# Node updates of a four-layer graph network: sums read over all banks, one root for two variances, a mask on one block, vector products of a fill by halves

## What is computed

```python
x = layernorm(x + mean of edge_attr_16 over the edges of each dst)
# L1: two passes with a small network on the edge attributes giving weights w
msg_s = einsum('ei,eij->ej', x[dst], wa) / 4;  msg_v = einsum('ei,eij,ec->ejc', x[dst], wb, sh1) / 4
out   = seg_mean(concat(msg_s, msg_v), src)              # 16 scalars and 4 vectors of 3 for each node
s0    = (out_s - mean) / sqrt(var + eps) * gs0 + bs0
v0    = out_v / sqrt(mean(out_v**2 over nodes, c) + eps) * gv0
msg   = (einsum(s0[dst], wa) + einsum(v0[dst] . sh1, wb) / sqrt(3)) / sqrt(20)
x     = layernorm(x + bn(seg_mean(msg, src)))
x     = layernorm(x + (leaky_relu(bn(seg_mean(x[src] @ W_e, dst) + x @ W_root + b)) + x))
x     = layernorm(x + tanh(gcn(tanh(gcn(x)))))
```

## Time and profile before

| | |
|---|---|
| median of three runs | 4055.97 us (4052.94 to 4059.43) |
| the profiled execution | 4055.89 us, its span 4054.2 us |
| TensorE busy | 3443.1 us, 85% |
| VectorE busy | 3345.4 us, 83% |
| GpSimd busy | 2800.4 us, 69% |
| ScalarE busy | 2652.3 us, 65% |

### The profile page before, as it was taken

The page is one execution under the profiler, slowest core; times in us unless marked ns, Lnnn a source line. Parts: engine busy times, 40 slices in busy tenths (PEclk is TensorE's granted clock), DMA queues, the critical chain, the costliest instruction groups (busy, mean ns, idle before and its releaser), DMA issues.

```text
span 4054.2 us, 105185 instructions
## 1 busy us (share of the span) xinstructions
PE 3443.1 (85%) x28557; PEld 2887.9 (71%) x28558; DVE 3345.4 (83%) x6593; ACT 2652.3 (65%) x3637; POOL 2800.4 (69%) x2751
## 2 busy tenths in 40 slices
PE   3559999999999699999999977778776888878887
PEld 3438888888888477777777766777775777757775
DVE  7789999999999688888888887888886787767876
ACT  2149999999999599999999960000002566745665
POOL 4447777777777377777777747776653777657774
PEclk9999999999999799999999988777776999989999
DMA  6011111111111321111111111111111222222221
GB/s 80 27 16 24 24 26 24 24 24 26 24 24 25 22 29 31 29 31 31 31 29 31 31 22 30 30 27 27 25 20 22 45 43 42 40 34 44 44 40 29
DMA packets 285654, 124.21 MB, mean 31 GB/s; under 512 B 179726, under 2 KB 260338, under 8 KB 285622
## 3 DMA queue, kind: packets, MB, share of 16 engines
q1 hardware_dynamic: 186838, 87.92, 9.4%
q0 software_dynamic: 84672, 29.47, 8.5%
q10 hardware_dynamic: 14112, 6.43, 0.7%
HBM read 121.80 MB, written 1.78 MB: 30 GB/s over the span
## 4 chain that ended last, share of the span: by engine, by line
PE 34%; issue 21%; POOL 20%; DVE 15%; DVEq 5%; DMA 3%; ACT 1%; POOLq 0%; SPq 0%; ACTq 0%
POOL gb L446 16%; PE ps L719 10%; PE ps L735 10%; PE ps L839 6%; POOL gb L436 3%; PE ps L725 2%; DVE oht L1283 2%; PE ps L633 2%; PE ps L855 2%; DVEq L284 2%; DVE oh L971 1%; DVE rest L987 1%; DMA eat<-vtab 1%; DVE xt L1099 1%; DMA gb<-table,idx 1%
## 5 line engine op out<-in xcount | busy, mean ns | idle before, releaser
L446 POOL DMA_INDIRECT gb<-table,idx x1568 | 1620.3, 1033 | 572.1 <-issue 451.3
L436 POOL DMA_INDIRECT gb<-table,idx x1078 | 1087.9, 1009 | 545.3 <-issue 453.4
L719 PE MATMUL ps<-big,oh 128*128 128x290 f32 (+1 forms) x7840 | 1264.6, 308 | 1.6 <-DVE big L1139 1.6
L719 PEld LDWEIGHTS ps<-big,oh 128*128 128x128 f32 x7840 | 1070.3, 191 | 124.9 <-DVE big L1139 2.2
L735 PE MATMUL ps<-w,ht 128*128 128x320 f32 x3136 | 1008.3, 444 | 123.9 <-DVE xt L1099 111.6
L546 ACT ACTIVATE oh<-iota_f,src_n 128x640 fp32r<-128x640 f32 x1372 | 1024.6, 815 | 0.0
L549 ACT ACTIVATE oh<-oh,ones 128x2560 fp32r<-128x2560 f32 (+1 forms) x392 | 849.6, 2167 | 12.8
L735 PEld LDWEIGHTS ps<-w,ht 128*128 128x128 f32 x3136 | 556.6, 191 | 384.4 <-DVE xt L1099 182.9
L1099 DVE TENSOR_TENSOR xt<-ps,gb 128x640 f32<-128x640 f32 x784 | 642.8, 820 | 77.0 <-PE ps L735 25.5
L599 ACT ACTIVATE rest<-rest,dst_f x1220 | 383.0, 389 | 321.0 <-PE ps L855 269.6
L1107 DVE TENSOR_REDUCE msg<-xt 128x80 f32<-128x1280 f32 (+1 forms) x392 | 580.3, 1480 | 0.0
(11 more groups left out here) (227 smaller groups left out, 2840.4 us busy)
## 6 DMA issues: line engine op xcount, KB each, us to landing
gb<-table,idx POOLq DMA_INDIRECT x2646, 2.4
eat<-in_eat SPq DMA_DIRECT2D x196, 192.0 KB, 2.4
eat<-vtab SPq DMA_DIRECT2D x98, 160.0 KB
eat<-vtab SPq DMA_DIRECT2D x49, 256.0 KB
eat<-vtab SPq DMA_DIRECT2D x98, 128.0 KB
rest<-in_edge_attr ACTq DMA_DIRECT2D x98, 64.0 KB, 1.8
idx<-in_src SPq DMA_DIRECT2D x245, 4.0 KB
idx<-in_dst SPq DMA_DIRECT2D x196, 4.0 KB
```

Source lines behind the costliest of these rows:

```text
L436: nc.gpsimd.indirect_dma_start(out=(gb if p == 2 else gr)[:, b, t, 0:tabw[p]], out_offset=None, in_=tabs[p], in_offset=bass.IndirectOffset ...
L446: nc.gpsimd.indirect_dma_start(out=gb[:, b, t, 0:tabw[p]], out_offset=None, in_=tabs[p], in_offset=bass.IndirectOffsetOnAxis(ap=idx[:, b, ...
L719: mm = nc.tensor.matmul(out, oh5[:, b, t, c * P:(c + 1) * P], big[:, b, t, 0:W], start=False, stop=False, skip_group_check=True)
```

## The change

The change has six parts. The sums after passes 0, 1 and 2 are read by instructions that span the banks, with one for the counts, one copy and one addition (two and two after pass 1, whose sums lie in two banks). The Newton step of a square root has four instructions, and the scaling of the mean in a layer norm is part of the subtraction. After pass 0 the vectors' sum of squares is taken together with the scalars' mean, and one root with 20 columns serves both variances. The mask is applied to block 24 alone. The constant factor of pass 1 is put into the inverse counts `rcs`, behind the store of the table of pass 0. In the first two steps of pass 1 the vector products are done by halves of four tiles.

```diff
@@ -492,7 +494,7 @@
             def stat_root():
-                root(sv_root[:, :], sv[:, 0:D])
+                root(sv_root[:, :], sv[:, 0:SW])
@@ -573,9 +575,7 @@
                 stat_root()
-                if l == 0:
-                    stat_root()
-                else:
+                if l == 1:
                     node_root()
@@ -764,10 +764,10 @@
                 nc.tensor.matmul(ps[:, 7, 0:32], zeros[:, 0:P], zeros[:, 0:32], start=True, stop=True).then_inc(s_accd, 1)
                 if l == 0:
-                    for k in range(3):
+                    for k in range(2):
                         partition_sum(k)
                 else:
-                    for k in range(3, 5):
+                    for k in range(2, 4):
                         partition_sum(k)
@@ -901,9 +901,8 @@
                 dve.wait_ge(s_sqo, k)
                 link(V.tensor_scalar(tmp, root, 1e-30, None, ALU.max))
                 link(V.reciprocal(tmp, tmp))
-                link(V.tensor_tensor(tmp, tmp, v, ALU.mult))
-                link(V.tensor_tensor(root, root, tmp, ALU.add))
-                link(V.tensor_scalar(root, root, 0.5, None, ALU.mult))
+                link(V.scalar_tensor_tensor(out=tmp, in0=tmp, scalar=0.5, in1=v, op0=ALU.mult, op1=ALU.mult))
+                link(V.scalar_tensor_tensor(out=root, in0=root, scalar=0.5, in1=tmp, op0=ALU.mult, op1=ALU.add))
@@ -990,8 +989,7 @@
             def layer_norm(xx):
                 link(V.tensor_reduce(r1[:, :], xx, AX.X, ALU.add))
-                link(V.tensor_scalar(r1[:, :], r1[:, :], 1.0 / D, None, ALU.mult))
-                link(V.tensor_tensor(xx, xx, bc(r1[:, :], D), ALU.subtract))
+                link(V.scalar_tensor_tensor(out=xx, in0=bc(r1[:, :], D), scalar=-1.0 / D, in1=xx, op0=ALU.mult, op1=ALU.add))
                 link(V.tensor_tensor(t2[:, :, 0:D], xx, xx, ALU.mult))
                 link(V.tensor_reduce(r1[:, :], t2[:, :, 0:D], AX.X, ALU.add))
                 roots[0] += 1
...
-            def batch_norm(xx, g, b_):
-
-                node_sum(xx, D)
+            def mask_nodes(xx):
+                last = xx[:, NB - 1, :]
+                link(V.tensor_tensor(last, last, mask[:, NB - 1:NB].broadcast_to([P, D]), ALU.mult))
+
+            def centred(xx):
                 link(V.tensor_scalar(sm[:, 0:D], ps[:, 5, 0:D], 1.0 / N, None, ALU.mult))
                 link(V.tensor_tensor(xx, xx, over_nodes(sm[:, 0:D], D), ALU.subtract))
-                link(V.tensor_tensor(xx, xx, bc(mask[:, :], D), ALU.mult))
+                mask_nodes(xx)
                 link(V.tensor_tensor(t2[:, :, 0:D], xx, xx, ALU.mult))
                 node_sum(t2[:, :, 0:D], D)
                 roots[0] += 1
                 V.tensor_scalar(sv[:, 0:D], ps[:, 5, 0:D], 1.0 / N, EPS, ALU.mult, ALU.add).then_inc(s_sqi, 1)
-                square_root(sv[:, 0:D], sv_root[:, :], sv_t[:, :], roots[0])
-                link(V.reciprocal(sv[:, 0:D], sv_root[:, :]))
+                square_root(sv[:, 0:SW], sv_root[:, :], sv_t[:, :], roots[0])
+                link(V.reciprocal(sv[:, 0:SW], sv_root[:, :]))
+
+            def scaled(xx, g, b_):
                 link(V.tensor_tensor(sv[:, 0:D], sv[:, 0:D], par[:, g, :], ALU.mult))
                 link(V.tensor_tensor(xx, xx, over_nodes(sv[:, 0:D], D), ALU.mult))
                 link(V.tensor_tensor(xx, xx, over_nodes(par[:, b_, :], D), ALU.add))
+
+            def batch_norm(xx, g, b_):
+                node_sum(xx, D)
+                centred(xx)
+                scaled(xx, g, b_)
@@ -1143,7 +1150,16 @@
                 def step(s, b, n, first):
                     prior = not (first and b == 0)
                     dve.wait_ge(gl_in[p][b][0], n * 16 * (T // 2))
-                    if l == 1:
+                    def first_vectors(h):
+                        rh = rhat[:, s, 4 * h:4 * h + 4, :]
+                        link(V.tensor_tensor(vprod[:, 4 * h:4 * h + 4, :, :],
+                                             gb[:, b, 4 * h:4 * h + 4, 0:12].rearrange("p t (j c) -> p t j c", c=3),
+                                             repeat(rh, 2, NV), ALU.mult))
+                        link(V.tensor_reduce(gb[:, b, 4 * h:4 * h + 4, 28:32], vprod[:, 4 * h:4 * h + 4, :, :], AX.X, ALU.add))
+
+                    if l == 1 and first:
+                        first_vectors(0)
+                    elif l == 1:
                         dve.wait_ge(gl_in[p][b][1], n * 16 * (T // 2))
                         rh = rhat[:, bass.ds(s, 1), :, :].rearrange("p o t c -> p (o t) c")
                         V.tensor_tensor(vprod[:, :, :, :], gb[:, b, :, 0:12].rearrange("p t (j c) -> p t j c", c=3),
@@ -1168,6 +1184,9 @@
                                     ALU.is_equal).then_inc(l_done[l], 1)
                     reduce_half(s, b, 0, first)
                     dve.wait_ge(gl_in[p][b][1], n * 16 * (T // 2))
+                    if l == 1 and first:
+                        first_vectors(1)
+                        dve.sem_inc(q_done[l], 2)
                     products_of(s, b, 2, first)
                     if l == 0:
                         vectors(s, b, 0)
...
-                    t1c = t1[:, :, :].rearrange("p (h c) f -> p h c f", c=NC)
-                    rcc = rcs[:, :].rearrange("p (h c) -> p h c", c=NC)
-                    for c in range(NC):
-                        av = ps[:, c, 0:NH * MP[0]].rearrange("p (h f) -> p h f", h=NH)
-                        link(V.tensor_scalar(rcc[:, :, c], av[:, :, MF], 1.0, None, ALU.max))
-                        link(V.tensor_copy(t1c[:, :, c, 0:MF], av[:, :, 0:MF]))
-                        link(V.tensor_tensor(t1c[:, :, c, 0:MF], t1c[:, :, c, 0:MF], av[:, :, MF + 1:2 * MF + 1], ALU.add))
+                    t1c = t1[:, :, :].rearrange("p (h c) f -> p c h f", c=NC)
+                    rcc = rcs[:, :].rearrange("p (h c) -> p c h", c=NC)
+                    av = ps[:, 0:NC, 0:NH * MP[0]].rearrange("p c (h f) -> p c h f", h=NH)
+                    link(V.tensor_scalar(rcc, av[:, :, :, MF], 1.0, None, ALU.max))
+                    link(V.tensor_copy(t1c[:, :, :, 0:MF], av[:, :, :, 0:MF]))
+                    link(V.tensor_tensor(t1c[:, :, :, 0:MF], t1c[:, :, :, 0:MF], av[:, :, :, MF + 1:2 * MF + 1], ALU.add))
                     link(V.reciprocal(rcs[:, :], rcs[:, :]))
                     link(V.tensor_tensor(rcs[:, :], rcs[:, :], mask[:, :], ALU.mult))
...
-                    batch_norm(tab[:, :, 12:MF], GS0, BS0)
+                    link(V.tensor_reduce(stat[:, 0:D], tab[:, :, 12:MF].rearrange("p q f -> p f q"), AX.X, ALU.add))
                     link(V.tensor_tensor(t2[:, :, 0:12], tab[:, :, 0:12], tab[:, :, 0:12], ALU.mult))
-                    node_sum(t2[:, :, 0:12], 12)
-                    link(V.tensor_copy(sm[:, 0:12], ps[:, 5, 0:12]))
-                    link(V.tensor_reduce(sv[:, 0:NV], sm[:, 0:12].rearrange("p (j c) -> p j c", c=3), AX.X, ALU.add))
-                    roots[0] += 1
-                    V.tensor_scalar(sv[:, 0:D], sv[:, 0:D], 1.0 / (3 * N), EPS, ALU.mult, ALU.add).then_inc(s_sqi, 1)
-                    square_root(sv[:, 0:D], sv_root[:, :], sv_t[:, :], roots[0])
-                    link(V.reciprocal(sv[:, 0:D], sv_root[:, :]))
-                    link(V.tensor_tensor(sv[:, 0:NV], sv[:, 0:NV], par[:, GV0, 0:NV], ALU.mult))
-                    link(V.tensor_copy(sm[:, 0:12].rearrange("p (j c) -> p j c", c=3), bc(sv[:, 0:NV], 3)))
+                    V.tensor_reduce(stat[:, D:MF], t2[:, :, 0:12].rearrange("p q f -> p f q"), AX.X, ALU.add).then_inc(s_str, 1)
+                    stats[0] += 1
+                    dve.wait_ge(s_sts, stats[0])
+                    link(V.tensor_reduce(sv[:, D:SW], ps[:, 5, D:MF].rearrange("p (j c) -> p j c", c=3), AX.X, ALU.add))
+                    link(V.tensor_scalar(sv[:, D:SW], sv[:, D:SW], 1.0 / (3 * N), EPS, ALU.mult, ALU.add))
+                    centred(tab[:, :, 12:MF])
+                    link(V.tensor_tensor(sv[:, D:SW], sv[:, D:SW], par[:, GV0, 0:NV], ALU.mult))
+                    link(V.tensor_copy(sm[:, 0:12].rearrange("p (j c) -> p j c", c=3), bc(sv[:, D:SW], 3)))
+                    scaled(tab[:, :, 12:MF], GS0, BS0)
                     V.tensor_tensor(tab[:, :, 0:12], tab[:, :, 0:12], over_nodes(sm[:, 0:12], 12), ALU.mult).then_inc(s_tabr, 1)
                     dve.sem_inc(s_node, 1)
+                    link(V.tensor_scalar(rcs[:, :], rcs[:, :], float(MJ) ** -0.5, None, ALU.mult))
...
-                    t1c = t1[:, :, :].rearrange("p (h c) f -> p h c f", c=NC)
-                    for c in range(NC):
-                        W5 = NH * MP[1]
-                        av = ps[:, c // 3, (c % 3) * W5:(c % 3 + 1) * W5].rearrange("p (h f) -> p h f", h=NH)
-                        link(V.tensor_copy(t1c[:, :, c, 0:D], av[:, :, 0:D]))
-                        link(V.tensor_tensor(t1c[:, :, c, 0:D], t1c[:, :, c, 0:D], av[:, :, D:2 * D], ALU.add))
```

(26 more changed lines are left out.)

## The result

The changed kernel takes 4044.5 us (median of 13 runs, 4042.36 to 4049.15) against 4057.23 us (13 runs, 4052.35 to 4060.39) for the kernel before on the same chip: a ratio of 0.9972, 95% interval 0.9965 to 0.9979, so 11.4 us less, between 8.5 and 14.2 (the two medians differ by 12.7). The profiled execution took 4042.56 us.

A forecast was written before the change was run, and what follows sets the result against it. Loops bound by TensorE (pass 0), GpSimd (pass 1), no single owner (pass 2); the change shortens VectorE stretches between them. Savings 1.24 + 5.49 + 2.58 + 2.96 + 0.43 = 12.70 us off 4055.97 gave 4043.3 us, range 4036 to 4051.

The forecast's parts named there:

- setup and first update: Before pass 0: shorter square roots and the layer norm's scaling taken out save 1.24 us.
- end of pass 0: Node update after pass 0: reading the sums saves 2.31 us, the statistics 3.18, together 5.49.
- fill of pass 1: First steps of pass 1: halves gain 0 us, GpSimd's index load ends it; rival gains up to 5.0, chance 0.12.
- end of pass 1: Node update after pass 1: wide reads, moved scaling, mask, root and layer norm save 2.58 us.
- end of pass 2: Node update after pass 2: wide reads, two masks, root and layer norm save 2.96 us.
- last update: End of the last pass: the layer norm saves 0.43 us.
- The reads: Ends of passes 0, 1, 2: fewer, wider instructions save 2.31, 1.13 and 1.52 us, with no price for spanning banks.
- The rival of half pace: Ends of passes 0, 1, 2: wide copies and adds cost double, 6.3 us more, 4049.6 us; chance 0.08.
- The statistics: End of pass 0: smaller mask, shorter root, one shared ones-matmul and one root for both variances save 3.18 us.
- The loss that the prediction took as its other bound: Fill of pass 1: an earlier 192 KB edge block load behind the index load costs about 1 us.
- The slower rival: Pass 2: TensorE's mean granted clock falls from 0.77 to 0.70, losing 23.4 us, 4066.7 us; chance 0.05.
- the way that the prediction put at 0.06: Loops of pass 1 or 2: transfers or waits fall differently and lose an earlier saving, 4050 us; chance 0.06.

The follow-up runs named there:

- e9: The changed kernel timed once more, unaltered, on a chip at the first result's speed: 4045.03 us, ratio 0.9968 to the kernel before.
- e10: The changed kernel without the halves in the fill of pass 1, vector products whole again: 4044.39 us, ratio 0.9969 to the kernel before.
- e11: The kernel before with only the reads over all banks after passes 0, 1 and 2: 4051.15 us, ratio 0.9985 to the kernel before.
- e4: The kernel before with only the statistics of pass 0 merged (one ones-matmul, one 20-column root), on a slower chip: ratio 0.998 to the kernel before.
- e12: The kernel before with only the statistics of pass 0 merged, on a chip at the first result's speed: 4059.95 us, ratio 1.0007 to the kernel before.
- e5: The changed kernel with indices of the third and fourth step of pass 1 loaded before the table's store: 4044.82 us, ratio 0.9965 to the kernel before.
- e6: The changed kernel with those indices of pass 1 loaded early as in e5, but without the halves: 4043.58 us, ratio 0.9961 to the kernel before.
- e8: The changed kernel with seven extra fills on VectorE ahead of pass 2's table copy, 15.8 us put in: 4061.48 us, ratio 1.0007 to the kernel before.
- e7: The changed kernel with pass 1's second edge block held until step 1's first four gathers landed: 4042.39 us, ratio 0.9961 to the kernel before.
- e1: The changed kernel without the halves in the fill of pass 1, on a slower chip: ratio 0.9984 to the kernel before.

## Why the prediction was right, by its steps

Predicted 4043.3 us, in a range of 4036 to 4051, and 12.70 us less; measured 4044.5, 11.4 less [8.5, 14.2], and 4045.03 when it was timed again. The range held it. The 1.2 us between the two times are the kernel before, 4055.97 us in the three runs that the prediction started from and 4057.23 in thirteen. By its terms, before against after in the trace:

| term | predicted | measured |
|---|---|---|
| setup and first update | 1.24 | 1.26 |
| end of pass 0 | 5.49 | 5.40 |
| fill of pass 1 | 0 | 0 within the variation, by e9 and e10 |
| end of pass 1 | 2.58 | 2.53 |
| end of pass 2 | 2.96 | 2.91 |
| last update | 0.43 | 0.42 |
| sum | 12.70 | 12.53 |

The first term's parts add up to 1.23 and not 1.24.

**The reads.** 2.08, 1.59 and 2.88 us, against 2.06, 1.60 and 2.88 predicted. The rival of half pace is out: a read over five banks costs its columns and nothing for the banks, and e11 shows the gain alone, 5.0 us in the trace with a ratio below 1. The Trainium skill, page "Advanced Engine Details and Errata", section "TRN2 Errata", lists that TRN2 can read several banks with one instruction; the trace agrees, and adds the price, 0.89 us for 700 columns.

**The statistics.** One wait of 0.73 us and one root fewer, as foretold; the stretches of e4 and e12 show 2.5 us for that part alone, though e12's time doesn't. I missed that the wider root serves pass 1 and 2 as well, 20 columns in place of 16 there too. In e12 that makes each of these two ends 0.04 to 0.05 us longer than before, which is what they fell short by in the change.

**The fill.** The term was right. The mechanism, that the index load and not VectorE holds GpSimd, is borne out by e5 and e6: only without the load's wait do the halves move the gathers, in one trace of each. Its details were off. VectorE began 6.7 us sooner after the store, not 5. I foresaw one wait at the seventeenth gather; with the halves there are two, in all three traces of that code (2.17 and 2.30 us in after, 2.15 and 0.91 in e9, 2.05 and 0.92 in e8), and one in the four kernels at this speed that have the index load late and no halves. VectorE's third step began 43.3 us after the store and not 42.7. The loss that the prediction took as its other bound, an edge block that comes early and is in the way, has something for it: with that block held back (e7) the second wait is gone. That is one trace, and the 25th gather starts at 39.2 us there against 39.6 to 41.0, so the size of the block's part is not settled. Little or nothing of it arrives at the sums: 1050.4 to 1051.0 us with the halves, 1050.5 to 1051.1 without.

**The slower rival.** TensorE's clock in pass 2 didn't answer: 0.77 in before, after, e8, e9, e10, e11 and e12, with starts from 2418 to 2436 us. The step was sound at this chip's speed. On the slower chip, at a mean of 0.61 in e1, TensorE was busy 654.54 us in pass 2, 180 more, and the loop 392 us longer; pauses (below) share in that, so it isn't the price of the clock alone.

**What the sum doesn't hold.** The rest, setup and loops, varied from 3908 to 3916 us over the ten profiles: two executions of the changed kernel differ by 3.8 us. Of the 13.2 us in the profiled span 0.7 is such variation. The loops of passes 0 and 2 lasted 1078.7 and 618.6 us against 1080.5 and 620.6 (the 601 us of the prediction are a stretch within the loop), so neither moved by what would have made the prediction wrong. Terms of 12.5 us stand out against all this; e12's 2.4 do not. That its loops took more than the updates gave back is the way that the prediction put at 0.06, a saving lost in a loop. In the whole change it didn't happen, and no step of the prediction says why not: there it had luck.

## What to carry to other kernels

In a stretch where one engine works and all others wait, an instruction that is taken out is worth its duration and its gap, and terms read from rows of the same shape came out within 0.1 us each. That holds for the stretch: the loops around it can take back more than a small term gives, as in e12. An earlier start on a consuming engine is worth nothing while its producer waits for something else: look at what the producer waits for, and remove that first. A part worth less than the loops' own variation is read from its own stretch of the trace, not from the whole time.
